# A GNN layer whose end stays in the turned layout: no turning back, variance by a matmul, t centred, the residual turned by VectorE between the panels

## The reference: what is computed

```python
h = jnp.maximum(_layernorm(x, axis=-1), 0.0)
# inside the layer, with ego_embeddings = h and res = h:
u = par_u[0] * par_u[1] * (diag_u[:, None] * ego_u @ W_u) + ego_u
i = par_i[0] * par_i[1] * (diag_i[:, None] * ego_i @ W_i) + ego_i
e = jnp.concatenate([u, i], axis=0)
h = adj @ (adj.T @ e)
mu = jnp.mean(h, axis=-1, keepdims=True)
var = jnp.var(h, axis=-1, keepdims=True)
out = (h - mu) * jax.lax.rsqrt(var + LN_EPS) * ln_gamma + ln_beta + res
x = x + out
```

## Time and profile before

| | us |
|---|---|
| median of 3 runs (382.1 to 383.28) | 382.22 |
| the profiled execution, its own time | 382.17 |
| its span, first to last instruction | 380.0 |
| PE busy in the span | 368.1 |
| DVE busy | 232.1 |
| ACT busy | 73.8 |
| POOL busy | 20.3 |

### The profile page before, as it was taken

How to read it: one execution, slowest core, us unless ns; L and a number is a source line. 1 busy time by engine, 2 the same in 40 slices (tenths; PEclk the granted TensorE clock), 3 DMA queues, 4 the chain that set the end, 5 groups by cost and what they waited for, 6 DMA issues and landing times.

```text
span 380.0 us, 9893 instructions
## 1 busy us (share of the span) xinstructions
PE 368.1 (97%) x4436; PEld 196.1 (52%) x4436; DVE 232.1 (61%) x205; ACT 73.8 (19%) x213; POOL 20.3 (5%) x28
## 2 busy tenths in 40 slices
PE   7999999999999999999999999999999999999991
PEld 3766455445643654465456436544644564365450
DVE  5997994669319912971693199139616931991057
ACT  5753111200220021022002200310220022003132
POOL 2029100000000000000000000000000000000013
PEclk9899999999999999999999999999999999999996
DMA  8999999999999999699959969995999699630003
GB/s 318 417 417 418 423 418 419 423 417 422 423 418 406 361 428 422 231 408 427 403 220 421 425 260 365 427 420 206 411 426 394 215 425 425 260 110 2 3 0 138
DMA packets 19025, 128.93 MB, mean 339 GB/s; under 512 B 2112, under 2 KB 2496, under 8 KB 3648
## 3 DMA queue, kind: packets, MB, share of 16 engines
q1 hardware_dynamic: 18720, 128.28, 82.3%
q10 hardware_dynamic: 288, 0.39, 0.3%
HBM read 127.36 MB, written 1.31 MB: 339 GB/s over the span
## 4 chain that ended last, share of the span: by engine, by line
PE 87%; DMA 7%; DVE 3%; SPq 2%; issue 0%; ACT 0%
PE t_acc L578 41%; PE h_acc L607 37%; PE h_acc L591 9%; DMA cols<-adj_cols 7%; SPq L191 1%; DVE scaled L532 1%; DVE var L397 1%; DVE scaled L528 1%; SPq L188 0%; PE t_acc L647 0%; DVE xs L535 0%; ACT squares L368 0%; DVE rstd L405 0%; SPq L199 0%
## 5 line engine op out<-in xcount | busy, mean ns | idle before, releaser
L434 DVE STREAM_TRANSPOSE strips<-natural 128x2048 f32<-128x2048 f32 x80 | 177.0, 2276 | 62.6 <-PE h_acc L607 62.6
L578 PE MATMUL t_acc<-natural,e 128*64 128x256 f32 x1600 | 176.2, 380 | 0.5 <-DMA natural<-adj_rows 0.5
L578 PEld LDWEIGHTS t_acc<-natural,e 128*64 128x64 f32 x1600 | 115.5, 137 | 62.4 <-issue 7.8
L607 PE MATMUL h_acc<-strips,centred 32*64 32x512 f32 x2560 | 140.1, 589 | 0.0
L607 PEld LDWEIGHTS h_acc<-strips,centred 32*64 32x64 f32 x2560 | 55.8, 132 | 83.1 <-issue 83.1
L314 ACT COPY t_high<-t_acc 64x256 f32<-64x256 f32 x20 | 7.4, 368 | 238.9 <-PE t_acc L578 238.9
L442 DVE TENSOR_TENSOR t_sum<-t_acc,t_high 64x256 f32<-64x256 f32 x20 | 8.2, 412 | 61.1 <-ACT t_high L314 60.8
L591 PE MATMUL h_acc<-cols,centred 128*64 128x512 f32 x160 | 38.3, 599 | 0.2 <-DMA cols<-adj_cols 0.2
L321 ACT COPY centred<-centred 32x384 f32<-32x384 f32 (+2 forms) x60 | 24.2, 403 | 39.2 <-DVE centred L447 38.7
L322 ACT COPY centred<-centred 32x128 f32<-32x128 f32 (+2 forms) x60 | 23.8, 397 | 0.0
L272 POOL TENSOR_TENSOR xs<-scaled,xs 128x512 f32<-128x512 f32 x4 | 5.1, 1268 | 331.6 <-DVE scaled L532 331.6
(11 more groups left out here) (39 smaller groups left out, 57.8 us busy)
## 6 DMA issues: line engine op xcount, KB each, us to landing
natural<-adj_rows SPq DMA_DIRECT2D x100, 1024.0 KB, 11.3
cols<-adj_cols SPq DMA_DIRECT2D x20, 1024.0 KB, 13.3
out<-xs SPq DMA_DIRECT2D x5, 256.0 KB, 2.0
xs<-x SPq DMA_DIRECT2D x3, 256.0 KB, 8.3
xs<-x ACTq DMA_DIRECT2D x1, 256.0 KB, 3.7
smalls<-small SPq DMA_DIRECT2D x1, 214.0 KB, 3.5
xs<-x ACTq DMA_DIRECT2D x1, 128.0 KB, 3.0
xs<-x SPq DMA_DIRECT2D x1, 128.0 KB, 2.8
```

Source lines behind the costliest of these rows:

```text
L434: nc.vector.transpose(strips[:, a, :, m].rearrange("p c t i -> p t c i"), natural[:, a, m].rearrange("p t (c j) -> p t c j", j=Q)).then_in ...
L578: last = nc.tensor.matmul(t_acc[D * s:D * (s + 1), a, 0:WIDE], e[:, GT * m + 2 * k + s, :], natural[:, a, m, HALF * s + k], start=(m == 0 ...
L607: last = nc.tensor.matmul(h_acc[D * s:D * (s + 1), q], t[part, a, b, u, :], rows, start=(isinstance(g, int) and g == 0 and b == 0 and u == 0),
```

## The change

- t is centred: `keep_t` adds two VectorE instructions between the transposes and the rise of `s_t_part`: a reduction of 32x512 to 32x8 sums, and a multiply-add that takes 1/64 of the sum off. So `h_acc` is centred and nothing is taken off at the end.
- The end keeps the turned layout. The copies and `out_turn` are gone. ScalarE squares a bank; TensorE sums the squares over the features with a 64x64 matrix of 1/64 (`out_var`), which leaves the variance repeated on all 64 partitions of its half; ScalarE takes the root of the bank, 128x512 values; VectorE takes the reciprocal of these 128x512 values and in one more instruction multiplies by gamma (now one value per partition) and by the reciprocal. The residual is added as before.
- The residual `xs` is turned by VectorE (`turn_residual`): 4 transposes of 32x512 after `keep_t(2)`, 8 after `keep_t(3)`, 4 after the last pair, and there 16 of 32x128 for bank 4. GpSimd's making of `centre` goes; a memset makes `mean`.
- The output is stored as (128, 5, 512), turned, and put in order on the host. Each store moves a 128x512 tile as before.

```diff
+            def out_square(b):
+                nc.scalar.activation(out_squares[:, b], h_acc[:, b], ACT.Square).then_inc(s_o_squares, 1)
+
+            def out_deviation(b):
+                act.wait_ge(s_o_var, b + 1)
+                nc.scalar.activation(out_rstd[:, b], var_bank(b), ACT.Sqrt, bias=eps[:]).then_inc(s_o_std, 1)
...
-            for half in range(2):
-                nc.scalar.copy(*strips_across(half, 0)).then_inc(s_o_low, 1)
-            square_out(0)
-            square_out(1)
+            out_square(0)
+            out_square(1)
+            out_square(2)
+            out_deviation(0)
+            out_square(3)
+            out_deviation(1)
+            out_deviation(2)
+            out_deviation(3)
             act.wait_ge(s_loaded_done, PANELS)
-            nc.scalar.copy(across[:, 0], h_acc[:, LOADED]).then_inc(s_o_loaded, 1)
-            for m in range(2, GROUPS):
-                square_out(m)
+            out_square(LOADED)
+            out_deviation(LOADED)
...
-                last.then_inc(s_t_part, 1)
+                last.then_inc(s_t_turned, 1)
+                rows = t[0:Q, a].rearrange("p b u d -> p (b u) d")
+                dve.wait_ge(s_t_turned, g + 1)
+                nc.vector.tensor_reduce(t_total[:], rows, AX.X, ALU.add).then_inc(s_t_total, 1)
+                dve.wait_ge(s_t_total, g + 1)
+                nc.vector.scalar_tensor_tensor(rows, t_total[:].unsqueeze(2).to_broadcast([Q, STRIPS, D]), -1.0 / D,
+                                               rows, ALU.mult, ALU.add).then_inc(s_t_part, 1)
...
+            def turn_residual(b):
+
+                if b == 0:
+                    dve.wait_ge(s_res, GROUPS)
+                    dve.wait_ge(s_dhw, LATER)
+                for q in range(QUADRANTS) if b == LOADED else (b,):
+                    for s in range(2):
+                        for d in range(D // Q):
...
+                            nc.vector.transpose(to, tiles).then_inc(s_res_turned, 1)
...
             for g in range(2, PAIRED):
                 step(g, g % 2, g // 2)
+                if g == 2:
+                    turn_residual(0)
+                else:
+                    turn_residual(1)
+                    turn_residual(2)
             pairs(dve, pair)
-            dve.wait_ge(s_strips_last, 1)
-            for half in range(2):
-                nc.vector.tensor_copy(*strips_across(half, 2)).then_inc(s_o_high, 1)
...
-                r = inverse_deviation(LATER + m)
-                dve.wait_ge(s_o_gamma, m + 1)
-                nc.vector.tensor_tensor(scaled[:, m % 2], scaled[:, m % 2], r, ALU.mult).then_inc(s_o_scaled, 1)
+            turn_residual(3)
+            turn_residual(LOADED)
+            dve.wait_ge(s_small, 16)
+            for b in range(GROUPS):
+                dve.wait_ge(s_o_std, b + 1)
+                nc.vector.reciprocal(out_rstd[:, b], out_rstd[:, b]).then_inc(s_o_rstd, 1)
+                dve.wait_ge(s_o_rstd, b + 1)
+                nc.vector.scalar_tensor_tensor(out_scaled[:, b], h_acc[:, b], gamma_s, out_rstd[:, b], ALU.mult,
+                                               ALU.mult).then_inc(s_o_scaled, 1)
...
-            def out_turn(m):
...
+            def out_var(b):
...
+                pe.wait_ge(s_o_squares, b + 1)
+                if b >= 3:
+                    pe.wait_ge(s_o_std, b - 2)
+                for s in range(2):
+                    half = slice(D * s, D * (s + 1))
+                    last = nc.tensor.matmul(var_bank(b)[half], mean[half], out_squares[half, b], start=True, stop=True)
+                last.then_inc(s_o_var, 1)
...
-            second_loaded(LAST - 1, 0, LAST // 2)
-            out_turn(0)
-            out_turn(1)
+            second_loaded(LAST - 1, 0, LAST // 2, range(1))
+            out_var(0)
+            out_var(1)
+            second_loaded(LAST - 1, 0, LAST // 2, range(1, BLOCKS))
+            out_var(2)
+            out_var(3)
             second_loaded(LAST, 1, LAST // 2)
-            for m in range(2, GROUPS):
-                out_turn(m)
+            out_var(LOADED)
```

More of the change, by code:

```diff
@@ L27 @@
 GAMMA = TILES + 4
[L28 removed]
+SMALL = GAMMA + 1 + D + 2 * P
 UNITS = ((0, 4), (4, 8), (8, 16), (16, 24), (24, 32), (32, 40))
@@ L60, in gnn_layer @@
         ident = sb("ident", [P, P])
-        centre = sb("centre", [P, P])
+        mean = sb("mean", [P, D])
         smalls = sb("smalls", [P, SMALL])
@@ L78, in gnn_layer @@
         across = sb("across", [P, 2, BANK])
-        h_across = natural[:, 0, 0].rearrange("p t c -> p (t c)").rearrange("p (m k q i) -> p m k q i", m=TURNED,
-                                                                            k=HALF, q=QUADRANTS)
+        out_squares, out_rstd, out_scaled = [
+            natural[:, a, m:m + 2].rearrange("p m t c -> p (m t c)").rearrange("p (b c) -> p b c", c=BANK)
+            for a, m in ((0, 0), (0, 2), (1, 0))]
+        t_total = sb("t_total", [Q, STRIPS])
         t_high = sb("t_high", [D, WIDE])
@@ L117, in gnn_layer @@
         s_t_sum = sem("s_t_sum")
+        s_t_turned = sem("s_t_turned")
+        s_t_total = sem("s_t_total")
         s_t_part = sem("s_t_part")
@@ L146, in firsts_0, with residual_bank, var_bank @@
             return (2, 4, 8, 9, 10)[m]
[L148 to L155, removed]
+        def residual_bank(b):
+            wide = (squares, squares, scaled, scaled)
+            if b == LOADED:
+                return across[:, 0]
+            return wide[b][:, b % 2].rearrange("p k d -> p (k d)")
+        def var_bank(b):
+            return (t_acc[:, 0], t_acc[:, 1], v_acc[:], t_acc[:, 0], t_acc[:, 1])[b]
         def rows_of(m):
@@ L246, in _ @@
                                     pattern=[[-1, P]], channel_multiplier=1).then_inc(s_ident, 1)
-            nc.gpsimd.memset(centre[:], 0.0).then_inc(s_zero, 1)
+            nc.gpsimd.memset(mean[:], 1.0 / D).then_inc(s_mean, 1)
             pool.wait_ge(s_small, 16)
@@ L261, in _ @@
                                         ALU.add).then_inc(s_res, 1)
[L262 to L272, removed]
+            pool.wait_ge(s_res_turned, 4 * LOADED)
+            for b in range(LOADED):
+                pool.wait_ge(s_o_scaled, b + 1)
+                nc.gpsimd.tensor_tensor(residual_bank(b), out_scaled[:, b], residual_bank(b),
                                         ALU.add).then_inc(s_o_added, 1)
@@ L462, in pair @@
                     keep_t(g + a, a)
+            def turn_residual(b):
[5 more added lines that the diff above has]
+                        for d in range(D // Q):
+                            part = slice(D * s + Q * d, D * s + Q * (d + 1))
+                            tiles = xs[Q * q:Q * (q + 1), rows_of(LOADED) if b == LOADED else slice(0, GT * TURNED),
+                                       Q * d:Q * (d + 1)].rearrange("p (k s) c -> p k s c", s=2)[:, :, s]
+                            to = residual_bank(b)[part]
+                            if b == LOADED:
+                                to = to.rearrange("p (k q i) -> p k q i", q=QUADRANTS, i=Q)[:, :, q]
+                            else:
+                                to = to.rearrange("p (k i) -> p k i", i=Q)
+                            nc.vector.transpose(to, tiles).then_inc(s_res_turned, 1)
             def deviation(u):
@@ L583, in first, with second_loaded @@
                     last.then_inc(s_first, 1)
[L585 to L589, removed]
+            def second_loaded(g, a, half, blocks=range(BLOCKS)):
+                if blocks[0] == 0:
+                    pe.wait_ge(s_cols[a], 16 * (half + 1))
+                    pe.wait_ge(s_t, g + 1)
+                for b in blocks:
                     for s in range(2):
@@ L594, in second_loaded @@
                                                 skip_group_check=True)
-                last.then_inc(s_loaded_done, 1)
+                if blocks[-1] == BLOCKS - 1:
+                    last.then_inc(s_loaded_done, 1)
             def second_strips(g, a):
@@ L631, in pair @@
                 second_loaded(g + 1, 1, half)
-            def out_turn(m):
-                if m == 0:
-                    pe.wait_ge(s_centre, 1)
+            def out_var(b):
+                if b == 0:
+                    pe.wait_ge(s_mean, 1)
                     pe.wait_ge(s_t_sum, PANELS)
[L638 to L648, removed]
+                pe.wait_ge(s_o_squares, b + 1)
[5 more added lines that the diff above has]
+                last.then_inc(s_o_var, 1)
             pe.wait_ge(s_idle, 1)
@@ L715 @@
         for d in range(2):
-            at = GAMMA + 2 * D + P * n + D * d
+            at = GAMMA + 1 + D + P * n + D * d
             small[D * d:D * (d + 1), at:at + D] = np.asarray(w)
-    small[:, GAMMA:GAMMA + D] = np.asarray(L0_gnn_ln_gamma)
-    small[:, GAMMA + D:GAMMA + 2 * D] = np.asarray(L0_gnn_ln_beta)
+    small[:, GAMMA] = np.tile(np.asarray(L0_gnn_ln_gamma), 2)
+    small[:, GAMMA + 1:GAMMA + 1 + D] = np.asarray(L0_gnn_ln_beta)
     arrays = {
```

49 lines of the change are left out of this document (19 added, 30 removed).

## The result

The changed kernel takes 391.73 us (median of 4 runs, 391.67 to 392.69) against 382.3 us (median of 4, 382.1 to 383.28): ratio 1.0247, 95% interval 1.0225 to 1.0268. It is slower by 9.4 us, where 8.7 were forecast (390.9). The profiled execution is the longest of the four, 392.69 us with a span of 390.9 us; the other three lie between 391.67 and 391.76, with spans of 389.9 to 390.0.

What follows compares the result with a forecast made beforehand. TensorE was taken to bound the panels and VectorE the end; -1.15 + 5 x (3.95 - 2.03) = +8.45, with +0.3 from panel 0 8.75 us on 382.17, gave 390.9 us, range 386.6 to 396.6.

Steps and rivals of the forecast that it cites:

- panel 0: First panel: centring delays the strips, TensorE waits before them and this stays to the end; +0.3 us.
- What bounds the kernel: TensorE sets the pace in the panels; VectorE sets it in the 12 us after the last strips.
- R: Time of one 128x512 VectorE reciprocal at the end, from small reciprocals' slope, 6.2 ns per element; 3.3 us.
- The end per bank: VectorE's reciprocal and multiply for each of five end banks: 3.95 us where it was 2.03.
- Ahead of VectorE's work: From last strips to VectorE's first reciprocal: copies and turn give way to square, out_var and root; -1.15 us.
- The cover in the panels: Centring and residual transposes on VectorE stay hidden beside TensorE in the panels after panel 0; nothing is paid.
- rival 3: Panels: 32-partition forms or strided transposes take twice as long, cover too thin; some 4 us more, 395 us; chance 0.05.
- rival 1: End: reciprocal makes eight passes, 8.3 ns per element, 4.4 us each; change +14.2, 396.4 us; chance 0.14.
- Rival 2: End: reciprocal streams like other instructions, 0.69 us, and TensorE sets the end; -3.0, 379.2 us; chance 0.06.

Runs made afterwards that it cites:

- no_reciprocal: The changed kernel without the five reciprocals of the end and their wait, banks multiplied by the root itself; 379.66 us, ratio 0.9928.
- before_centred: The kernel before with only the centring of t added (reduction and multiply-add per panel), end unaltered; 382.93 us against 382.28, ratio 1.0014.
- centred_twice: The changed kernel with the centring of t done twice in each panel; 396.68 us, ratio 1.0373.
- fewer_residual_turns: The changed kernel without the twelve transposes of the residual after panels 2 and 3; 392.11 us, ratio 1.0259.
- one_root_gpsimd_late: The changed kernel with root and reciprocal as one ScalarE instruction per bank, and GpSimd's additions of beta held until panel 0's centring is done; 379.27 us.

## Why the prediction was right, point by point

- **The number.** 390.9 us forecast, 391.73 measured, and part of that closeness is luck. In the span the forecast was +8.75 us and the profiled pair shows +10.9: the terms below are short by 1.3 (panel 0), 0.5 (the five banks) and 0.4 us (ahead of them). It comes to only 0.8 us in the time because the middle executions are about 1 us shorter than the profiled one, and because 0.4 us more fell away outside the span, which the forecast knew nothing of.
- **What bounds the kernel.** Right. TensorE to the last strips, VectorE after them; `no_reciprocal` shows that work on VectorE in the end counts in full, `before_centred` that in the panels it hardly counts.
- **R.** 3.3 us forecast, 3.345 measured, and 6.25 ns per element between 256 and 512 columns against the 6.2 taken. Taking the first of the small reciprocals out was decisive: with it, R would have been 2.7 us and the forecast 3 us lower. Two instructions that differ by four elements are thin evidence, and each ns between two such rows moves R by 0.13 us. The single pairs gave 2.0 to 3.4 us, so that 3.3 came out this close is in part luck too.
- **The end per bank.** 3.95 us forecast, 4.05 measured: R is 0.05 longer, and the multiply takes 0.75 rather than 0.69. Five banks make 0.5 us of the difference.
- **Ahead of VectorE's work.** -1.15 us forecast, -0.76 measured, each part a little long: the half of `second_loaded` 1.01 rather than 0.93, `out_var` 1.03, the root 0.70 rather than 0.6.
- **Panel 0.** The place was right, the term was mis-sized, and the larger wait was not the one it named: 0.3 us forecast, 1.6 in the profiled execution, 0.65 in the median time of `before_centred`. The forecast looked at the strips, which are late by 0.20, and called the spread just in time. Without a hold the spread is late by 0.34 (`fewer_residual_turns`, `one_root_gpsimd_late`), and the strips start 0.4 to 0.6 us later than before; with the hold of 0.95 it is late by 1.29. The forecast gave the multiply-add 0.69 us without looking at what GpSimd does at that moment.
- **The cover in the panels, and rival 3.** Right that the cover holds and that rival 3 is out: pairs pay nothing, the residual's 32x512 transposes take 0.70 us as forecast, and dropping twelve changes nothing. `centred_twice` found the edge at panels 3 and 4, where the room was put at 2.1 us; at panel 3 it is about 1 us more.
- **Rivals 1 and 2.** Neither: six times the multiply-add's cost per element, not eight times or once. Rival 2's time of 379.2 us is near what the kernels without VectorE's reciprocal measured, 379.66 and 379.81, and the path over TensorE and ScalarE that it worked out is the one that the profile shows. Its length was not right: from the end of the last strips to that of the last add it had 11.3 us, 0.7 of them a reciprocal, and `no_reciprocal` took 11.6 with none (376.69 less 365.06), so the other steps take 1.0 us longer than it gave them (two `out_var` 1.9 us, for one, where it had 1.7); that the times agree so well is luck. The Trainium skill ("VectorE: DVE Perf Modes", section "First, the fixed hardware budget") gives the reciprocal a repeat count of 8 and no time. Read as eight passes per element, with rival 1's estimate, that would be 4.4 us; the trace, at 3.345 us, does not bear this reading out.

## What to carry to other kernels

A layout that saves a turn can make a small vector wide: here 128x8 reciprocals became 128x512, and an operation that costs six times the multiply-add per element ate a gain of 2.6 us more than four times over. Before such a change, look for the operation whose count of elements grows, price it by the slope between two sizes in the trace, and see whether another engine makes the result on its way, as ScalarE did here at no cost. Work put beside a saturated engine is free only where the consumer comes later than the result: check the first steps, where the pipeline is not yet full, one by one, and look at what GpSimd is doing when VectorE must read two tiles in SBUF.

## What the hardware showed that was not expected

- VectorE's reciprocal in float32 costs 6.25 ns per element (1746 ns at 128x256, 3345 ns at 128x512), six times the multiply-add's 1.04.
- The multiply-add of the centring, which has two inputs in SBUF, is held by a running GpSimd addition until that ends: 0.68 us became 0.76 to 1.63 in nine profiles, always ending 0.53 to 0.56 us after GpSimd's instruction, and GpSimd's next one took 1.54 instead of 1.08 us. No run looks at other forms.
- ScalarE's reciprocal root from PSUM costs 0.69 us for 128x512, no more than its square root.
- GpSimd's additions of beta fell from 1.27 to 1.09 us in the changed kernel, where the instruction is the same and beta lies at another place in its tile; no run looks into this.
